# Weight splits over blocks, last stores awaited one stage later, an earlier table load: the seams of a four-stage kernel

## Chip, cores and metric

The kernel runs on one core of a Trainium2 chip. The metric is the time of one execution on the device, in microseconds; lower is better. Five engines work side by side, each through its own list of instructions in order: TensorE (PE, with PEld for its weight loads), VectorE (DVE), ScalarE (ACT), GpSimd (POOL) and SyncE (SP, which here only issues transfers). ACT issues transfers too. They wait for one another by semaphores.

## The reference, cut to what matters

```python
x = x + 0.5 * ffn(layernorm(x))        # base projection + 2 of 8 low-rank experts
x = x + attention(layernorm(x))        # 32 heads, 8 key/value heads, rotary, causal
x = x + 0.5 * ffn(layernorm(x))
...
q = (resid @ Wq)...; k = (resid @ Wk)...; v = (resid @ Wv)...
q = q * cos + _rotate_half(q) * sin
k = k * cos + _rotate_half(k) * sin
att = einsum(q, k) / sqrt(32); causal softmax; ctx = probs @ v
return out @ Wo
```

`x` is 2 x 1024 x 1024 in float32: 2,048 tokens, 16 tiles of 128 tokens. All weights are 1024 wide, Wk and Wv 256 wide.

## The kernel before, in words

Every product is made of float32 operands split in a high and a low part: ACT copies the operand into the type that TensorE takes (the high part), DVE or POOL subtracts it from the original (the low part), and `split_products` (L73) issues three matmuls: high x high, low x high, high x low.

The kernel is four stages in a row, each a `Block` whose end all engines reach before the next one starts:

1. `ffn_stage` "f1" (L100) reads `x`, writes `x1` to memory tile by tile. SP issues the store of a tile (L331) when DVE has added the last part, and at the stage's end (L337) waits until all stores have landed. The first four tiles are also loaded again and normalised into the buffer `early`, and Wq is split.
2. `qkv_stage` "qkv" (L779) computes queries, keys and values in four chunks of 512 tokens (batch b, chunk ch). PE first turns the four early tiles (L959), then `by_pairs` (L965) makes the blocks o = 0 and 1 of the first chunk in two halves of 256 tokens. After that, per chunk: ten output blocks o = 0 to 9 (eight of queries, two of keys) of 24 matmuls each, then four tiles of values. In the blocks o = 1, 3, 5, 7 PE turns a tile of the next chunk at the end of the block (L959, `turn_h`); for that the tile must have been loaded by SP (`load_x`, L894), measured by DVE (L1160, L1164), given its deviation by ACT (L1035) and normalised by DVE (L1172). ACT makes the high part of the turned tile (L1040), DVE the low part (L1178). Each output block passes DVE (L1222, L1224), POOL (L1136), DVE (L1183), ACT (L1047) and POOL (L1130), and ACT stores both parts to memory (L1059). PE needs a bank back after DVE's L1224, four blocks later.
3. `attention_stage` "at" (L1238): sixteen passes of scores, exponentials on ACT (L1670), sums and products.
4. `ffn_stage` "f2" reads `x1` and the attention's result and writes the output.

Wk and Wv are needed from block o = 8 of the first chunk (PE waits for all eight pieces, L1001). Their eight pieces go through two raw buffers (`wkv_raw`): SP loads a piece when POOL is done with the piece two before it (L925 to L927), ACT makes the high part (L1075), POOL the low part (L1124). All eight stand in front of everything else of the stage on ACT and POOL, except that ACT first makes the high parts of the four early tiles:

```python
for j in range(KC):
    act.wait_ge(wkv_loaded[j % WRAW], 32 * (j // WRAW + 1))
    act.activation(wkv_hi[:, j, :], wkv_raw[:, j % WRAW, :], ACT.Copy).then_inc(wkv_hi_done, 1)
```

At the end of the stage, ACT copies each value tile (L1104) and stores it (L1064), calls an exponential on one column so that its table is loaded (L1113), and waits for all stores of queries, keys and values (L1115, L1116).

## Time and profile before

| | us |
|---|---|
| median of 3 runs | 1552.35 (1551.92 to 1552.43) |
| profiled execution | 1550.97 |
| its span, first to last instruction | 1549.2 |
| PE busy in the span | 1504.8 |
| first stage, to about | 260.4 |
| queries, keys, values, to about | 570.2 |
| attention, to about | 1137.6 |
| last stage, to | 1549.2 |

All times below are in microseconds from the span's start. A busy PE counts from the start of a matmul to its modelled end, so starts are the safer thing to compare. "PEq L108" as a releaser stands for the point at which all engines meet at the end of a stage. "Issue" means that the profile shows nothing that the engine waited for.

### The profile page before, as it was taken

How to read it: one execution, taken by the hardware profiler on the slowest of the kernel's cores; microseconds unless marked ns; L12 is line 12 of the kernel's file. 1: busy time of each engine (PE TensorE's matmuls, PEld its weight loads, DVE VectorE, ACT ScalarE, POOL GpSimd, SP SyncE). 2: the span in 40 equal slices, each digit the busy share in tenths (PEclk: the TensorE clock that was granted, in tenths of full speed). 3: DMA queues.
4: the chain of work that ended last, by engine and by line, in shares of the span. 5: the costliest groups of instructions: out<-in, count | busy, mean ns of one | idle time of the engine just before them, and what ended most of it. 6: DMA issues, size and time to landing. Idle time of an engine off the chain costs nothing. (4 is left out here: it accounts for less than half of the span.)

```text
span 1549.2 us, 25938 instructions
## 1 busy us (share of the span) xinstructions
PE 1504.8 (97%) x9184; PEld 1189.7 (77%) x9184; DVE 957.6 (62%) x2726; ACT 569.0 (37%) x1058; POOL 696.2 (45%) x384
## 2 busy tenths in 40 slices
PE   7999998899999989999999999999999999999999
PEld 7999998788888875555555555555479999898988
DVE  6645464465563848888888888888655434343423
ACT  4323233221211136566565556566632212121210
POOL 1322222443334338888888888888612101010100
PEclk9999999999999989999999999999999999999999
DMA  6332324333415172433333344430161212121201
GB/s 234 126 123 86 125 97 147 114 133 98 136 69 158 70 180 53 100 84 82 77 77 76 77 96 101 101 84 23 49 238 48 82 42 82 42 81 41 82 14 41
DMA packets 118725, 146.01 MB, mean 94 GB/s; under 512 B 40896, under 2 KB 77120, under 8 KB 118336
## 3 DMA queue, kind: packets, MB, share of 16 engines
q1 hardware_dynamic: 90304, 121.37, 27.2%
q10 hardware_dynamic: 28304, 23.14, 4.5%
q8 instruction: 66, 1.08, 0.3%
q14 instruction: 51, 0.42, 0.1%
HBM read 95.72 MB, written 53.51 MB: 96 GB/s over the span
## 5 line engine op out<-in xcount | busy, mean ns | idle before, releaser
L1670 ACT ACTIVATE at_probs<-ps 128x512 f32<-128x512 f32 (+1 forms) x640 | 307.1, 557 | 146.2 <-PE ps L1585 145.9
L69 DVE CUSTOM_DVE_ANT_0 ps<-ps,at_score_mask 128x512 f32<-128x512 f32 (+2 forms) x480 | 271.7, 620 | 58.7 <-PE ps L1574 58.1
L348 POOL TENSOR_TENSOR f_x_ring<-f_x_ring,f_half_bias 128x1024 f32<-128x1024 f32 x32 | 78.2, 2445 | 309.3 <-DVE f_h L634 303.1
L1517 POOL TENSOR_TENSOR at_added<-at_added,at_probs 128x2048 f32<-128x2048 f32 (+1 forms) x60 | 210.4, 3506 | 2.2
L1602 PE MATMUL ps<-at_probs,at_vs 128*32 128x512 f32 (+3 forms) x1536 | 157.0, 496 | 0.0
L75 PE MATMUL f_ps<-f_wt_hi,f_hT_hi 128*128 128x400 f32 (+1 forms) x384 | 133.3, 347 | 3.3 <-DVE f_hT_lo L638 3.3
L75 PE MATMUL ps<-f_wt_hi,f_hT_hi 128*128 128x400 f32 (+1 forms) x384 | 131.5, 342 | 0.0
L77 PE MATMUL f_ps<-f_wt_hi,f_hT_lo 128*128 128x400 f32 (+1 forms) x384 | 130.9, 341 | 0.0
L76 PE MATMUL f_ps<-f_wt_lo,f_hT_hi 128*128 128x400 f32 (+1 forms) x384 | 130.6, 340 | 0.0
L76 PE MATMUL ps<-f_wt_lo,f_hT_hi 128*128 128x400 f32 (+1 forms) x384 | 130.2, 339 | 0.0
L77 PE MATMUL ps<-f_wt_hi,f_hT_lo 128*128 128x400 f32 (+1 forms) x384 | 130.0, 338 | 0.0
L69 DVE CUSTOM_DVE_ANT_0 ps<-ps,at_score_mask,at_part_max 128x128 f32<-128x128 f32 (+3 forms) x240 | 120.3, 551 | 1.3 <-issue 0.8
L1497 POOL TENSOR_SCALAR_AFFINE_SELECT at_probs<-at_probs 128x512 f32<-128x512 f32 (+1 forms) x96 | 79.4, 827 | 73.5 <-ACT at_probs L1670 73.5
L673 DVE TENSOR_TENSOR f_x_ring<-ps,f_x_ring 128x512 f32<-128x512 f32 x32 | 21.8, 689 | 138.4 <-PE ps L77 125.1
L1585 PE MATMUL ps<-heads 98*128 98x512 f32 (+3 forms) x288 | 96.7, 383 | 6.4 <-PEq L1557 3.9
L75 PE MATMUL ps<-wide_hi,shared 128*128 128x512 f32 x256 | 101.1, 395 | 1.5 <-DVEq L703 1.0
L1136 POOL TENSOR_TENSOR qkv_rot<-qkv_rot,qkv_sin 128x512 f32<-128x512 f32 x40 | 51.6, 1291 | 111.5 <-DVE qkv_rot L1222 111.5
L77 PE MATMUL ps<-wide_hi,shared 128*128 128x512 f32 x256 | 99.8, 390 | 0.0
L76 PE MATMUL ps<-wide_lo,shared 128*128 128x512 f32 x256 | 99.7, 390 | 0.0
L1585 PEld LDWEIGHTS ps<-heads 98*128 98x128 f32 x288 | 52.9, 196 | 56.2 <-ACT at_probs L1670 30.6
L352 POOL TENSOR_TENSOR wide_lo<-f_wq_raw,wide_hi 128x512 f32 (+1 forms) x16 | 23.6, 1474 | 158.3 <-ACT wide_hi L531 158.3
L1047 ACT ACTIVATE qkv_rope_hi<-qkv_rope 128x512 fp32r<-128x512 f32 x40 | 25.3, 632 | 184.5 <-DVE qkv_rope L1183 171.9
(202 smaller groups left out, 3600.0 us busy)
## 6 DMA issues: line engine op xcount, KB each, us to landing
f_x_ring<-in_L_attn_resid SPq DMA_DIRECT2D x16, 512.0 KB, 3.4
x<-f_x_ring SPq DMA_DIRECT2D x16, 512.0 KB, 2.7
early<-x SPq DMA_DIRECT2D x16, 512.0 KB, 3.3
scr_q_hi<-qkv_rope_hi ACTq DMA_DIRECT2D x32, 256.0 KB, 2.0
scr_q_lo<-qkv_rope_lo ACTq DMA_DIRECT2D x32, 256.0 KB, 2.3
scr_ctx<-at_ctxn SPq DMA_DIRECT2D x32, 256.0 KB, 2.4
shared<-scr_ctx SPq DMA_DIRECT2D x16, 512.0 KB, 4.5
f_x_ring<-x SPq DMA_DIRECT2D x16, 512.0 KB, 3.7
```

The costliest lines, as they stand in the source:

```text
L69: return dve.tensor_tensor_reduce(out=src[:, 0:keys], in0=src[:, 0:keys], in1=mask, scale=1.0, scalar=part_max[:, g, own] if c else -3.0e3 ...
L75: pe.matmul(out, stat_hi, mov_hi, start=start, stop=False)
L76: pe.matmul(out, stat_hi, mov_lo, start=False, stop=False)
L77: return pe.matmul(out, stat_lo, mov_hi, start=False, stop=stop)
L348: pool.tensor_tensor(x_ring[:, u, :], x_ring[:, u, :], half_bias[:], ALU.add).then_inc(bias_added, 1)
L1047: act.activation(rope_hi[:, g % 2, :], rope[:, g % 2, :], ACT.Copy).then_inc(hi_done, 1)
L1136: pool.tensor_tensor(rot[:, g % 2, :], rot[:, g % 2, :], sin[:, cols], ALU.mult).then_inc(sin_done, 1)
L1497: pool.affine_select(out=tile, in_=tile, compare_op=ALU.is_ge, fill=0.0, base=0, pattern=[[0, G], [0, count], [1, P]], channel_multiplier= ...
L1517: pool.tensor_tensor(added[:, heads, :], first, probs[:, (NU * n + u) % PROBS, heads, :], ALU.add).then_inc(added_done, 1)
L1585: last = pe.matmul(score_ps[x % BANKS][:, cols], ks[:, nm, j * P:(j + 1) * P], q_stack(n)[0:KROWS + 2, half, g, at], start=True, stop=True)
L1602: last = pe.matmul(ctx_ps[g * DH:(g + 1) * DH, at], vs[:, n % RING, j, :], probs[:, (NU * n + u) % PROBS, g, cols], start=j == 0, stop=u i ...
L1670: act.activation(probs[:, (NU * n + u) % PROBS, g, cols], score_ps[x % BANKS][:, cols], ACT.Exp, scale=SCALE).then_inc(exp_done, 1)
```

## The change

- The pieces of Wk and Wv are split in the blocks of the first chunk, by ACT and by POOL: pieces 0 and 1 ahead of block o = 0, piece o + 1 ahead of block o, up to o = 6. SP loads tiles 6 and 7 between the pieces 3 and 4 and the pieces 5 and 6 (before: after piece 7).
- The store of the last tile of stage 1 counts on a semaphore of its own (`x_stored`), for which SP waits as its first act in stage 2. `x_ring` is given another place in the memory.
- ACT no longer waits for the value stores at the end of stage 2; SP waits for them in stage 3, after its first three loads. `v_out` outlives the stage.
- The exponential on one column is called ahead of the four value tiles of the last chunk (before: after them).
- Loops of one round are written out.

```diff
--- before.py
+++ after.py
@@ -97,7 +97,7 @@
     return tile[:, :, :].rearrange("p c n -> p (c n)") if len(tile.shape) == 3 else tile[:, :]
-def ffn_stage(nc, name, x_src, x_dst, base_b, consts, ident, chunk_loaded, prep=None, attn=None):
+def ffn_stage(nc, name, x_src, x_dst, base_b, consts, ident, chunk_loaded, prep=None, attn=None, x_stored=None):
@@ -112,6 +112,7 @@
         def sem(n):
             return ctx.enter_context(nc.semaphore(f"{name}_{n}"))
+        x_ring = sb("x_ring", [P, 4, D], F32)
         fw = ffn_weights(nc, ctx, name)
         (wt_hi, wt_lo), (bt_hi, bt_lo) = fw["wt"], fw["bt"]
         if prep:
@@ -126,7 +127,6 @@
         if attn:
             wo_hi, wo_lo = attn["wo"]
             ctxT = [attn["ctxT"][:, par, :, :, :] for par in range(2)]
-        x_ring = sb("x_ring", [P, 4, D], F32)
         half_bias = sb("half_bias", [P, D], F32)
         h = sb("h", [P, D], F32)
         hT_hi = sb("hT_hi", [P, 2, KC, P], F32R)
@@ -328,13 +328,14 @@
                     sp.dma_start(prep["copy"]["wt"][bass.ds(2 * i + u // 2, 1), half, :].rearrange("c p n -> (c p) n"),
                                  prep["ffn_w"][bass.ds(2 * i + u // 2, 1), half, :].rearrange("c p n -> (c p) n")).then_inc(copy_stored, 16)
                 sp.wait_ge(ffn_added, 3 * t + 6)
-                sp.dma_start(x_dst[bass.ds(t * P, P), :], x_ring[:, u, :]).then_inc(stored[u], 16)
+                own = x_stored if prep and isinstance(t, int) and t == NT - 1 else stored[u]
+                sp.dma_start(x_dst[bass.ds(t * P, P), :], x_ring[:, u, :]).then_inc(own, 16)
             if prep:
                 for u in range(2):
                     step(0, u, u, 3)
             run_tiles(sp, step)
             for s in range(4):
-                sp.wait_ge(stored[s], 16 * (NT // 4) + (16 if s == 3 else 0))
+                sp.wait_ge(stored[s], 16 * (NT // 4) + (16 if s == 3 and not prep else 0))
             if prep:
                 sp.wait_ge(copy_stored, 16 * (1 + NT))
@@ -776,7 +777,7 @@
             run_tiles(dve, step)
-def qkv_stage(nc, x_src, wq, early, heads, w, consts, ident, scr):
+def qkv_stage(nc, x_src, wq, early, heads, v_out, w, consts, ident, scr, x_stored, v_stored):
@@ -813,7 +814,6 @@
         rope = sb("rope", [P, 2, HALF], F32)
         rope_hi = sb("rope_hi", [P, 2, HALF], F32R)
         rope_lo = sb("rope_lo", [P, 2, HALF], F32R)
-        v_out = sb("v_out", [P, 2, KV], F32)
@@ -857,7 +857,6 @@
         out_stored = [sem(f"out_stored{s}") for s in range(2)]
         v_done = sem("v_done")
         v_copied = sem("v_copied")
-        v_stored = [sem(f"v_stored{s}") for s in range(2)]
         first_head_loaded = sem("first_head_loaded")
         rest_loaded = sem("rest_loaded")
         mask_ready = sem("mask_ready")
@@ -882,11 +881,15 @@
         def run_chunks(eng, step):
-            with eng.Fori(0, B - 1, 1) as b:
+            for b in range(B):
                 for ch in range(NCH):
-                    step(b, ch, True)
-            for ch in range(NCH):
-                step(B - 1, ch, ch + 1 < NCH)
+                    step(b, ch, b + 1 < B or ch + 1 < NCH)
+
+        def weights_of(b, g):
+
+            if b or g >= KC - 1:
+                return ()
+            return (0, 1) if g == 0 else (g + 1,)
         @block.sync
         def _(sp):
@@ -914,6 +917,7 @@
                     dst = q_stacks[0][KROWS + row:KROWS + row + 1, half * G:(half + 1) * G, :].rearrange("p g t -> p (g t)")
                     sp.dma_start(dst.bitcast(F32), src).then_inc(neg_loaded, 16)
+            sp.wait_ge(x_stored, 16)
             sp.dma_start(cos[:], consts["rope_cos"]).then_inc(const_loaded, 16)
             sp.dma_start(sin[:], consts["rope_sin"]).then_inc(const_loaded, 16)
             for j in range(KC):
@@ -921,13 +925,14 @@
                     sp.wait_ge(h_turned, TC + 1)
                     for slot in range(2):
                         load_x(TC + slot, slot)
+                if j in (WRAW + 2, WRAW + 4):
+                    load_x(TC + j // 2, j // 2 % 2)
                 if j >= WRAW:
                     sp.wait_ge(wkv_lo_done, j - WRAW + 1)
                 for cols, src in ((slice(0, KV), w["Wk"]), (slice(KV, 2 * KV), w["Wv"])):
                     sp.dma_start(wkv_raw[:, j % WRAW, cols], src[j * P:(j + 1) * P, :]).then_inc(wkv_loaded[j % WRAW], 16)
-            with sp.Fori(TC // 2 + 1, NT // 2, 1) as i:
-                for slot in range(2):
-                    load_x(2 * i + slot, slot)
+            for t in range(TC + 4, NT):
+                load_x(t, t % 2)
             sp.wait_ge(v_done, (B * NCH - 1) * TC + 1)
             for s in range(2):
                 sp.wait_ge(out_stored[s], NCH * NO * 16 + 16)
@@ -1070,7 +1075,8 @@
             act.wait_ge(eps_set, 1)
             for t in range(TC):
                 high_hT(0, t, early=True)
-            for j in range(KC):
+
+            def high_weight(j):
                 act.wait_ge(wkv_loaded[j % WRAW], 32 * (j // WRAW + 1))
                 act.activation(wkv_hi[:, j, :], wkv_raw[:, j % WRAW, :], ACT.Copy).then_inc(wkv_hi_done, 1)
@@ -1086,6 +1092,8 @@
                 act.wait_ge(v_done, b * (NCH * TC) + (ch * TC + 1))
                 for o in range(NO):
                     g = ch * NO + o
+                    for j in weights_of(b, g):
+                        high_weight(j)
                     if not more and o and TURN_A in items_of(o):
                         negative(0)
                     if more and o % 2 == 0 and o // 2 < TC:
@@ -1097,6 +1105,8 @@
                     if more and o % 2 == 1 and o // 2 < TC:
                         high_hT(b, (ch + 1) * TC + o // 2)
+                if not more:
+                    act.activation(std[:], eps[:], ACT.Exp)
                 for s in range(TC):
                     t = ch * TC + s
                     act.wait_ge(v_done, b * (NCH * TC) + (t + 2))
@@ -1110,19 +1120,19 @@
                         negative(1)
                     store_v(b, t)
             run_chunks(act, step)
-            act.activation(std[:], eps[:], ACT.Exp)
             for s in range(2):
                 act.wait_ge(out_stored[s], B * NCH * NO * 16 + 16)
-                act.wait_ge(v_stored[s], B * NCH * TC * 8 + 16)
         @block.gpsimd
         def _(pool):
             pool.memset(eps[:], EPS).then_inc(eps_set, 1)
             pool.sem_inc(lo_done, 2)
-            for j in range(KC):
+
+            def low_weight(j):
                 pool.wait_ge(wkv_hi_done, j + 1)
                 pool.tensor_tensor(wkv_lo[:, j, :], wkv_raw[:, j % WRAW, :], wkv_hi[:, j, :].bitcast(F32),
                                    ALU.subtract).then_inc(wkv_lo_done, 1)
+
             pool.wait_ge(const_loaded, CONSTS)
             def low_part(b, g):
@@ -1131,6 +1141,8 @@
                                    ALU.subtract).then_inc(lo_done, 1)
             def chunk_step(b, g):
+                    for j in weights_of(b, g):
+                        low_weight(j)
                     cols = slice((g // NO) * HALF, (g // NO + 1) * HALF)
                     pool.wait_ge(swapped, b * (NCH * NO) + (g + 1))
                     pool.tensor_tensor(rot[:, g % 2, :], rot[:, g % 2, :], sin[:, cols], ALU.mult).then_inc(sin_done, 1)
@@ -1139,7 +1151,7 @@
                     if g % NO == NO - 1:
                         low_part(b, g)
-            with pool.Fori(0, B - 1, 1) as b:
+            for b in range(B - 1):
                 for g in range(NCH * NO):
                     chunk_step(b, g)
             for g in range(NCH * NO):
@@ -1235,7 +1247,7 @@
             run_chunks(dve, step)
-def attention_stage(nc, consts, ident, scr, wo, wo_src, heads, shared, ps):
+def attention_stage(nc, consts, ident, scr, wo, wo_src, heads, shared, ps, v_stored):
@@ -1453,6 +1465,8 @@
             for r in range(2):
                 sp.sem_inc(stacks_loaded[r], LOADS - 16)
                 load_v(r)
+            for stored in v_stored:
+                sp.wait_ge(stored, NT * 8 + 16)
             for stored in ctx_stored:
                 sp.sem_inc(stored, 16)
@@ -1793,15 +1807,19 @@
     chunk_loaded = [whole.enter_context(nc.semaphore(f"chunk_loaded{c}")) for c in range(KC + 1)]
     wide = [whole.enter_context(nc.sbuf_tensor(f"wide_{part}", [P, KC, D], F32R)) for part in ("hi", "lo")]
     over = ExitStack()
+    x_stored = whole.enter_context(nc.semaphore("x_stored"))
+    v_stored = [whole.enter_context(nc.semaphore(f"v_stored{s}")) for s in range(2)]
     with ExitStack() as ctx:
         early = ctx.enter_context(nc.sbuf_tensor("early", [P, 4, D], F32))
-        ffn_stage(nc, "f1", x, x1, base_b, consts, ident, chunk_loaded, prep={"wq": wide, "early": early, "Wq": ins["L0_attn_Wq"], "copy": copy, **raw})
+        ffn_stage(nc, "f1", x, x1, base_b, consts, ident, chunk_loaded, prep={"wq": wide, "early": early, "Wq": ins["L0_attn_Wq"], "copy": copy, **raw},
+                  x_stored=x_stored)
         heads = over.enter_context(nc.sbuf_tensor("heads", [P, 2, KC, HALF], F32R, side="right"))
-        qkv_stage(nc, x1, wide, early, heads, attn_w, consts, ident, scr)
+        v_out = over.enter_context(nc.sbuf_tensor("v_out", [P, 2, NKV * DH], F32, side="right"))
+        qkv_stage(nc, x1, wide, early, heads, v_out, attn_w, consts, ident, scr, x_stored, v_stored)
     with ExitStack() as ctx:
         shared = ctx.enter_context(nc.sbuf_tensor("shared", [P, 2, 2, KC, P], F32R))
         ps = ctx.enter_context(nc.psum_tensor("ps", [P, 8, HALF], F32))
-        attention_stage(nc, consts, ident, scr, wide, ins["wo_rows"], heads, shared, ps)
+        attention_stage(nc, consts, ident, scr, wide, ins["wo_rows"], heads, shared, ps, v_stored)
         over.close()
         ffn_stage(nc, "f2", x1, y, base_b, consts, ident, chunk_loaded,
                   attn={"wo": wide, "ctxT": shared, "ps": ps, "ffn_w": copy["wt"], "ffn_bt": copy["bt"],
```

## Rows read from the trace of the kernel before

**Rows 1.** The page: granted clock in tenths, 40 slices.

```profile
PEclk9999999999999989999999999999999999999999
```

**Rows 2.** Timeline of PE, 257 to 296 us: start, us, instruction, [idle before <-releaser].

```profile
259.19 0.27 PE L77 MATMUL f_ps<-f_bt_hi,f_lowT_lo 128*128 128x224 f32 x1
...
263.62 5.35 PE L959 MATMUL qkv_ps<-ident,early 128*128 128x128 f32 x32 [4.16 <-PEq L108]
...
269.40 0.39 PE L75 MATMUL qkv_ps<-heads,wide_hi 128*128 128x256 f32 x1 [0.43 <-DVE heads L1178]
...
280.90 0.28 PE L77 MATMUL qkv_ps<-heads,wide_lo 128*128 128x256 f32 x1
...
288.38 1.94 PE L959 MATMUL qkv_ps<-ident,early 128*128 128x128 f32 x8 [7.19 <-issue]
```

**Rows 3.** Windows: length, PE, PEld, DVE, ACT, POOL busy, PEclk, DMA, GB/s.

```profile
264.00:264.50 0.50, 0.50 (x5) 0.50 (x4) 0.00 (x0) 0.00 (x0) 0.00 (x0) 0.50 0.50 66
...
267.00:267.50 0.50, 0.50 (x6) 0.50 (x5) 0.50 (x1) 0.43 (x1) 0.00 (x0) 0.71 0.97 377
...
291.00:292.00 1.00, 1.00 (x5) 0.83 (x4) 1.00 (x1) 0.00 (x0) 0.52 (x1) 0.91 0.07 25
```

**Rows 4.** Timelines of DVE and ACT at the first normalised tile.

```profile
272.26 1.28 DVE L1160 BATCH_NORM_STATS2 qkv_stats<-early 128x6 f32<-128x512 f32 x2 [0.65 <-DMA early<-x]
...
286.81 1.47 DVE L1172 TENSOR_SCALAR early<-early,qkv_mv,qkv_rstd 128x1024 f32<-128x1024 f32 x1
...
286.29 0.28 ACT L1035 ACTIVATE qkv_std<-qkv_mv,qkv_eps 128x1 f32<-128x1 f32 x1
```

**Rows 5.** Groups of ACT by line, and timeline of POOL, 262 to 290 us.

```profile
L1075 ACT ACTIVATE qkv_wkv_hi<-qkv_wkv_raw 128x512 fp32r<-128x512 f32 x8 | 4.9, 632 | 11.5 <-DMA qkv_wkv_raw<-in_L_attn_Wv 11.5
...
280.24 2.50 POOL L1124 TENSOR_TENSOR qkv_wkv_lo<-qkv_wkv_raw,qkv_wkv_hi 128x512 fp32r<-128x512 f32 x2 [2.47 <-ACT qkv_wkv_hi L1075]
```

**Rows 6.** Timeline and waits of the queue of SP, 225 to 300 us.

```profile
260.07 0.35 SPq L331 DMA_DIRECT2D x<-f_x_ring  x1
...
SPq L337 <- DMA x<-f_x_ring: 2.3, 1, 2.3
```

**Rows 7.** Timelines of DVE and PE at a later turned tile.

```profile
322.74 0.81 DVE L1172 TENSOR_SCALAR early<-early,qkv_mv,qkv_rstd 128x1024 f32<-128x1024 f32 x1
...
325.96 1.03 PE L959 MATMUL qkv_ps<-ident,early 128*128 128x128 f32 x8
```

**Rows 8.** Timelines of PE and ACT, 535 to 578 us.

```profile
561.03 0.28 PE L75 MATMUL qkv_ps<-qkv_wkv_hi,qkv_hT 128*128 128x256 f32 x1
...
566.67 0.28 PE L77 MATMUL qkv_ps<-qkv_wkv_hi,qkv_hT 128*128 128x256 f32 x1
...
570.84 4.18 PE L1585 MATMUL ps<-heads 98*128 98x512 f32 x10 [3.89 <-PEq L1557]
...
558.64 0.39 ACT L1104 ACTIVATE qkv_v_out<-qkv_ps 128x256 f32<-128x256 f32 x1 [0.43 <-PE qkv_ps L77]
...
567.40 0.38 ACTq L1064 DMA_DIRECT2D scr_v<-qkv_v_out  x1
...
567.81 1.28 ACT L1113 ACT_TABLE_LOAD   x1 [0.44 <-ACT qkv_v_out L1104]
```

**Rows 9.** Timeline of PE, 570 to 582 us, and one window.

```profile
574.82 0.41 PE L1574 MATMUL ps<-heads,wide_lo 96*128 96x128 f32 x1
...
581.00:581.50 0.50, 0.50 (x3) 0.48 (x2) 0.38 (x2) 0.46 (x2) 0.50 (x1) 0.68 1.22 280
```

**Rows 10.** Timeline of PE and windows in the first 60 us.

```profile
13.21 0.43 PE L75 MATMUL f_ps<-f_wt_hi,f_hT_hi 128*128 128x360 f32 x1 [2.37 <-DVE f_hT_lo L638]
...
57.43 0.30 PE L434 MATMUL f_ps<-ident,f_low_s 128*128 128x128 f32 x1 [1.68 <-DVE f_hT_lo L638]
...
15.00:16.50 1.50, 1.50 (x6) 1.50 (x6) 1.35 (x4) 0.56 (x3) 0.00 (x0) 0.50 0.69 158
...
58.50:60.00 1.50, 1.50 (x10) 1.50 (x9) 1.27 (x3) 0.89 (x2) 0.00 (x0) 1.00 0.00 0
```

## Prediction

> **What bounds the kernel now.** I read the page first. PE is busy 1504.8 of 1549.2 us, 97%, and the granted clock is 9 tenths or more in 39 of the 40 slices; the one with an 8 is the fifteenth, 542 to 581 us, and holds a seam [rows 1]. So a change that does not shorten PE's own work can only gain where PE stands still or runs at the lower clock. The waits of PE name few places, and I went to the timeline of PE around them. At the seam between the first and the second stage the last matmul starts at 259.19 and ends at 259.46, and the first transpose starts at 263.62: 4.16 us of nothing. Then come 32 transposes, a pause of 0.43, the pair blocks from 269.40 to 281.18, and then a second hole of 7.19 us before the transposes at 288.38 [rows 2]. The windows show the clock. It is at half (1.2 of 2.4 GHz) at 264.0 and is given back inside 267.0 to 267.5; it is at half again after the second hole and comes back early in the window 291 to 292, whose mean is 0.91 [rows 3]. At the seam between the second and the third stage PE stands still from 566.95 to 570.84 [rows 8], and the clock is then at half until inside 581.0 to 581.5 [rows 9]. The seam to the last stage has no such wait, and between the seams the waits of PE name nothing of size. Time won at a seam is therefore kept: everything behind it is PE's own chain, moved to the left.
>
> **The second hole (edit 1).** PE stands at the turning of tile 4. Who is late? DVE measured that tile at 272.26, as soon as it was loaded, but could normalise it only at 286.81, because ACT gave the deviation at 286.29 [rows 4]. ACT was busy with the eight weight pieces: eight copies of 632 ns are 4.9 us, and it waited 11.5 us for their loads in between, since each load waits for POOL to free a buffer, 1.25 us a piece [rows 5]. In the new order only pieces 0 and 1 stand ahead of the deviation. Both had landed when ACT reached them before. The deviation then follows the measuring, which ends at about 273.8 even if the tile is loaded no sooner than now; with 0.3 for ACT, 0.2 for a reciprocal and 0.8 for the normalising, the tile stands at about 275.3. PE needs it at 277.5 or later (below). The hole goes: 7.2 us.
>
> The tail goes with it. From 288.38 to 291.1 PE worked at half clock, 2.7 us in which it did 1.35 us of work [rows 2, 3]: 1.4 us.
>
> What the eight pieces cost in their new place: per block 0.63 us more of ACT, 1.25 more of POOL. A block lasts PE about 5.9 us by the two pair blocks, which take 11.8. POOL has two more operations of about the same length in it, so 3.8 of 5.9; ACT has far less. Both sit ahead of the block's own waits, where POOL stands idle for DVE. Queued behind them are the sine product on POOL, and on ACT the deviation and the high part of the turned tile, which PE needs for the next turn. I looked for how much room that loop has: tile 7's normalising starts at 322.74, is done at 323.55, and PE turns it at 325.96 [rows 7]. That is 2.4 us of room, and one ACT copy plus one POOL piece is 1.9 if nothing of them hides. I count them at nothing; without cover they would still fit. Piece 7 is done in block 6, a whole block before PE asks for it. The loads of tiles 6 and 7, now between the pieces, make SP wait for the normalised tiles 4 and 5 before it loads pieces 4 and 6; the first is ready at about 275, the second a block later, and a piece has about two blocks between POOL's release and ACT's use.
>
> **The first seam (edit 2).** SP issues the last store at 260.07, is through with it at 260.42, and waits 2.3 us until it lands; PE starts at 263.62, 0.9 us after that [rows 2, 6]. SP's waits name this store alone there; all others were issued with the tiles before. Without the wait, PE starts 0.9 us after 260.42, at 261.3: 2.3 us. The wait itself moves to SP in stage 2, where cosine, sine, pieces 0 and 1 and tiles 4 and 5 queue behind it. SP's first transfer therefore starts at about 262.8 and no later than now, and what hangs on it (tile 4, needed by 277.5) has the room shown above. Bounds: 0, if something else is as late as the store, and 2.3. I take 2.3, since the row names the store.
>
> PE's hole is then 259.46 to 261.3, 1.8 us. Does the clock fall? This kernel has two holes near that size: after 2.37 us (up to 13.21) the clock was at half in 15.0 to 16.5, after 1.68 us (up to 57.43) it stayed full [rows 10]. 1.8 is nearer to the second, so I take full clock. The transposes then take 1.03 for eight where they take 1.94 at half [rows 2, 7]. The pair blocks wait for the first two of the four tiles to be split, so the gain is at least one such difference, 0.9, and at most two, 1.8: 1.3 us. The pair blocks then start at 265.7 and end at 277.5, 11.8 later as now. If the clock falls after all, the 1.3 is lost, and as much half clock as at this seam now (264 to 267.3 [rows 3]) costs up to 1.7 more.
>
> **The second seam (edits 3 and 4).** ACT issues the last value store at 567.40 for 0.38 us, loads the table from 567.81 to 569.09, and waits for the store. PE starts at 570.84 [rows 8]. Both the table and the landing must leave this place to gain anything, and both do. ACT arrives at 567.8; with the 0.9 of the first seam PE starts at 568.7, with a little more for the different first instructions at 568.8: 2.0 us. Bounds 0 and 2.2. The moved table load takes 1.28 and its column 0.2 in front of the copy at 558.64 [rows 8], which then ends at about 560.4. The third value tile, which takes that bank again, starts at 561.03 [rows 8], so it is free. SP waits for the value stores behind three loads, and nothing that it issues after them is due in the first pass.
>
> The Trainium skill, "ScalarE: Activation LUTs", section "What ACT_TABLE_LOAD costs", counts a drain on top of the load, 2.66 us in all. By that figure the copy would end at about 561.8, PE would stand still for some 0.8, and the sum would be 13.9 in place of 14.7. The row shows the activation right behind the 1.28 us.
>
> How long is the clock at half in attention? Now until 581.3. PE is paced by ACT up to 574.82 and works without pause from there [rows 9], so half clock costs at most half of 6.5 us, 3.2. The hole shrinks to 1.9 us, but matmuls paced by ACT follow it, unlike the two cases above. Bounds 0 and 3.2; I think it falls mostly as now and take 0.5.
>
> **Sum.** 7.2 + 1.4 + 2.3 + 1.3 + 2.0 + 0.5 = 14.7 us. The profiled execution took 1550.97, so 1536.3, with a span of 1534.5. The median lies 1.4 above the profiled one: 1537.6.
>
> **Rivals.**
> - *Full clock at both seams:* the 0.5 becomes 3.2, and with the bounds of the rest the gain is 17.6: 1534.7. For it: both holes shrink below 2 us. Against it: the fall after 2.37 [rows 10]. The Trainium skill, "TensorE: Matmul & The Clock Gate", section "HAM oscillation — how this bites in real kernels", has the clock fall only after idle gaps longer than both of these. By that rule this rival is the forecast, 1534.7; the fall after 2.37 us speaks against taking it whole. 15%.
> - *The clock falls at the first seam as well:* 14.7 less 3.0 is 11.7: 1540.7. 15%.
> - *Something else holds the seams:* the stores are not what the engines wait for last, and 2.3 and 2.0 are lost: 1541.9. Against it: the wait of SP is 2.3 long and names the store. 8%.
> - *Half a hole stays:* tile 4 is still late, by a load that starts later or a piece that has not landed: 3 to 5 us, 1541 to 1543. 5%.
> - *Slower:* the pieces no longer run as a batch, and each puts its load on PE's path. The loop tile, deviation, normalise, turn has 2.4 us of room. From there on every block pays. ACT waited about 3 us for a landing; with 0.6 and 1.25 for the splits that is 4.9 a block, less 1.2 of room, over seven blocks 26: 1552.35 - 14.7 + 26 = 1563.6; it decides from 2.1 a block on (14.7 over seven). Against it: a piece has two blocks of time to land. 3%.
>
> The forecast itself, 1536 to 1539.5, gets 54%. The range from 1534.5 to 1542 holds that and the first three rivals, over 8 in 10. A measurement of this kernel can tell about 0.2%, 3.1 us, from no change. Faster by more than that: 0.95; within it: 0.02; slower: 0.03.
>
> **What would show it.** In the profile of the changed kernel: no wait of PE at the turning of tile 4, the transposes there directly behind the pair blocks; PE's holes at the seams 1.8 and 1.9 us; transposes of about 1.03 for eight at the first seam; POOL and ACT splitting weights up to about 310, with no PE wait between. A PE wait at a turn or at the first key block, a first transpose later than 262, or a half clock in the pair blocks would make me wrong.

## The result, and the profile after

The changed kernel takes 1538.83 us in the median of four runs (1536.21 to 1541.13), and the kernel before, on the same chip, 1552.13 (1551.16 to 1552.43). The ratio is 0.9915, with a 95% interval of 0.9894 to 0.9936: 13.3 us faster. The predicted time was 1537.6. The profiled execution took 1536.89 with a span of 1535.1, against a forecast of 1536.3 and 1534.5.

First, PE's timeline of the changed kernel, at the first seam and at the turns of tiles 4, 5 and 7 (start, us, instruction, idle time before it):

```profile
258.12 0.27 PE L77 MATMUL f_ps<-f_bt_hi,f_lowT_lo 128*128 128x224 f32 x1
260.31 5.35 PE L964 MATMUL qkv_ps<-ident,early 128*128 128x128 f32 x32 [1.92 <-PEq L108]
265.42 0.36 PE L75 MATMUL qkv_ps<-heads,wide_hi 128*128 128x256 f32 x1
...
276.90 0.29 PE L77 MATMUL qkv_ps<-heads,wide_lo 128*128 128x256 f32 x1
277.02 1.03 PE L964 MATMUL qkv_ps<-ident,early 128*128 128x128 f32 x8
...
289.12 1.04 PE L964 MATMUL qkv_ps<-ident,early 128*128 128x128 f32 x8
...
313.30 1.04 PE L964 MATMUL qkv_ps<-ident,early 128*128 128x128 f32 x8
```

The page's row of the granted clock, beside [rows 1], has no slice below 9 any more:

```profile
PEclk9999999999999999999999999999999999999999
```

PE's timeline set beside [rows 2]: the hole at the seam is 1.92 us where it was 4.16, and the second hole, 7.19 us before the turn of tile 4, has gone; the eight transposes stand directly behind the last matmul of the pair blocks and take 1.03, not 1.94. But the 32 transposes at the seam take 5.35 us, as before. The windows say why (length, busy time of PE, PEld, DVE, ACT and POOL, granted clock, DMA share, GB/s):

```profile
261.00:261.50 0.50, 0.50 (x6) 0.50 (x5) 0.00 (x0) 0.02 (x1) 0.00 (x0) 0.82 0.24 90
261.50:262.00 0.50, 0.50 (x5) 0.50 (x4) 0.00 (x0) 0.50 (x1) 0.00 (x0) 0.50 0.00 0
...
264.50:265.00 0.50, 0.50 (x6) 0.50 (x5) 0.50 (x1) 0.24 (x1) 0.00 (x0) 0.77 1.03 410
...
558.00:558.50 0.50, 0.50 (x2) 0.25 (x1) 0.00 (x0) 0.50 (x2) 0.00 (x0) 0.78 1.26 197
558.50:559.00 0.50, 0.50 (x2) 0.29 (x1) 0.00 (x0) 0.50 (x3) 0.00 (x0) 0.50 1.16 183
...
565.00:565.50 0.50, 0.50 (x5) 0.26 (x2) 0.00 (x0) 0.00 (x0) 0.00 (x0) 0.89 1.14 225
```

A window whose mean lies between 0.50 and 1.00 holds the change of level. The clock was at half from 261.3 to 264.7 and from 558.3 to 565.1. DVE and ACT at the first normalised tile, which answer to [rows 4, 5]:

```profile
272.35 0.21 DVE L1176 BATCH_NORM_AGGREGATE qkv_mv<-qkv_stats 128x2 f32<-128x12 f32 x1
...
273.12 0.81 DVE L1184 TENSOR_SCALAR early<-early,qkv_mv,qkv_rstd 128x1024 f32<-128x1024 f32 x1
...
267.28 1.22 ACT L1081 ACTIVATE qkv_wkv_hi<-qkv_wkv_raw 128x512 fp32r<-128x512 f32 x2 [0.55 <-DMA qkv_wkv_raw<-in_L_attn_Wv]
272.60 0.29 ACT L1040 ACTIVATE qkv_std<-qkv_mv,qkv_eps 128x1 f32<-128x1 f32 x1 [4.10 <-DVE qkv_mv L1176]
272.81 0.63 ACT L1081 ACTIVATE qkv_wkv_hi<-qkv_wkv_raw 128x512 fp32r<-128x512 f32 x1
```

ACT now waits for DVE's measuring and gives the deviation 0.04 us after it ends (272.56). Tile 4 is normalised at 273.93, and PE turns it at 277.02. The other pieces follow one a block; POOL's eighth starts at 307.37. SP's queue at the first seam, its timeline and then its waits, beside [rows 6]:

```profile
259.00 0.35 SPq L332 DMA_DIRECT2D x<-f_x_ring  x1
261.65 0.34 SPq L921 DMA_DIRECT2D qkv_cos<-in_rope_cos  x1
...
265.70 0.81 SPq L900 DMA_DIRECT2D early<-x  x2
```

```profile
SPq L921 <- DMA x<-f_x_ring: 1.6, 1, 1.6
```

The wait for the last store is now SP's alone: it lands at 261.65, when PE has been at work for 1.3 us. The second seam, PE and ACT, beside [rows 8]:

```profile
554.30 0.28 PE L77 MATMUL qkv_ps<-qkv_wkv_hi,qkv_hT 128*128 128x256 f32 x1
556.56 0.93 PE L1599 MATMUL ps<-heads 98*128 98x512 f32 x3 [1.98 <-PEq L1571]
...
546.12 1.28 ACT L1109 ACT_TABLE_LOAD   x1 [0.27 <-ACT qkv_rope_hi L1052]
547.41 0.20 ACT L1109 ACTIVATE qkv_std<-qkv_eps 128x1 f32<-128x1 f32 x1
547.52 0.37 ACT L1114 ACTIVATE v_out<-qkv_ps 128x256 f32<-128x256 f32 x1
...
555.03 0.38 ACTq L1069 DMA_DIRECT2D scr_v<-v_out  x1
```

The hole went from 3.89 to 1.98 us, and the table load lies among the value tiles.

Measured between the same instructions of PE, the two profiled executions differ by this ledger:

| stretch | before | after | gain | predicted |
|---|---|---|---|---|
| start to the last matmul of stage 1 | 259.19 | 258.12 | 1.1 | 0 |
| to the first transpose | 4.43 | 2.19 | 2.2 | 2.3 |
| to the first pair matmul | 5.78 | 5.11 | 0.7 | 1.3 |
| to the turn of tile 4 | 18.98 | 11.60 | 7.4 | 7.2 |
| to the turn of tile 5 (301.81; 289.12) | 13.43 | 12.10 | 1.3 | 1.4 |
| to the last matmul of stage 2 | 264.86 | 265.18 | -0.3 | 0 |
| to the first score | 4.17 | 2.26 | 1.9 | 2.0 |
| to the last products of attention (1125.15; 1110.44) | 554.31 | 553.88 | 0.4 | 0.5 |
| to the end | 424.05 | 424.66 | -0.6 | 0 |
| sum | 1549.2 | 1535.1 | 14.1 | 14.7 |

### The profile page after: what moved, and what is told of

It reads as the page before. It is cut to its first block and busy times, and to the rows that moved or that the text cites. A ratio compares the mean times of both kernels' runs of the same rounds, so it can differ in the third digit from the quotient of the medians.

```text
span 1535.1 us, 25888 instructions
## 1 busy us (share of the span) xinstructions
PE 1501.5 (98%) x9184; PEld 1186.6 (77%) x9184; DVE 957.4 (62%) x2726; ACT 568.7 (37%) x1058; POOL 697.3 (45%) x384
## 3 DMA queue, kind: packets, MB, share of 16 engines
q8 instruction: 66, 1.08, 0.3%
```

## The experiments

All are timed against the kernel before on the same chip, with four to six runs of each version. Gains by the ratio are (1 - ratio) x 1552; the ratio rests on all runs, so it can differ from the ratio of the two medians by up to a thousandth and a half, 2 us. For the three parts of the change both are given.

**The same kernel again.** No edit.

> The changed kernel once more, against the kernel before on the same chip. Theory A (each part is worth the piece of PE's standstill that it removes; the clock at the seams is decided anew in each run): 1536 to 1541, ratio 0.990 to 0.993, single runs up to 4 us apart, where the kernel before has 1. Theory B (one state of the chip, slower or faster for the whole job): the runs of this kernel lie within 1 us of each other, as those of the kernel before do.

1539.31 us, ratio 0.9913 (0.9894 to 0.9933), single runs from 1536.59 to 1544.24. The profiled one took 1540.42, span 1538.7, 3.6 longer than the first profile. Its windows:

```profile
559.50:560.00 0.50, 0.50 (x2) 0.27 (x2) 0.00 (x0) 0.50 (x2) 0.00 (x0) 0.53 0.94 172
...
572.50:573.00 0.50, 0.50 (x3) 0.41 (x2) 0.50 (x1) 0.28 (x1) 0.00 (x0) 0.50 0.00 0
573.00:573.50 0.50, 0.50 (x3) 0.43 (x2) 0.41 (x3) 0.34 (x2) 0.00 (x0) 0.81 0.00 0
```

Half clock lasts from 559.5 to 573.2 here, 13.7 us, where the first profile has 6.8. The ledger puts 3.5 of the 3.6 us into attention (557.38 for 553.88). Another 1.1 come from stage 1 (last matmul at 259.21, not 258.12), and other stretches give back 1.0. So identical code differs by several us, most of it from how long the clock stays at half. The mean granted clock that each timed run of this kernel left says the same without a profile: the five runs at 0.995 to 0.997 took 1536.21 to 1538.21 us, the five at 0.992 to 0.994 took 1540.42 to 1544.24.

The median lies in A's range and B is refuted, but A's "up to 4 us apart, where the kernel before has 1" is not borne out: the single runs lie 7.7 us apart, and those of the kernel before on this chip 7.1 (1550.54 to 1557.66). On this chip the spread is no property of the change.

**The split alone**, with both seams as before:

```diff
-                own = x_stored if prep and isinstance(t, int) and t == NT - 1 else stored[u]
-                sp.dma_start(x_dst[bass.ds(t * P, P), :], x_ring[:, u, :]).then_inc(own, 16)
+                sp.dma_start(x_dst[bass.ds(t * P, P), :], x_ring[:, u, :]).then_inc(stored[u], 16)
...
-                sp.wait_ge(stored[s], 16 * (NT // 4) + (16 if s == 3 and not prep else 0))
+                sp.wait_ge(stored[s], 16 * (NT // 4) + (16 if s == 3 else 0))
...
-            sp.wait_ge(x_stored, 16)
...
-                if not more:
-                    act.activation(std[:], eps[:], ACT.Exp)
...
+            act.activation(std[:], eps[:], ACT.Exp)
             for s in range(2):
                 act.wait_ge(out_stored[s], B * NCH * NO * 16 + 16)
+                act.wait_ge(v_stored[s], B * NCH * TC * 8 + 16)
```

> The weight splits over the blocks alone; the last store, the value stores and the table load as in the kernel before. Theory A: the second hole of 7.2 us and its half-clock tail of 1.4 go, so 1543.6 (8.6 less than before), with PE's holes at the two seams at 4.2 and 3.9 us as before. Theory C (the splits cost something in their new place, on ACT or POOL): less than 7 us gained, and PE waits at a turn of a tile between 277 and 330. Theory D (all of the gain is in the splits, the seams are worth nothing): as fast as the changed kernel, 1538 to 1539.

1546.16 us, ratio 0.9958 (0.9943 to 0.9973); the profiled run took 1543.3. The holes of the seams are back at 4.16 and 3.90 us, and PE has none at the turn of tile 4. From the first pair matmul to that turn it takes 11.6, as in the full change. The row of the turn has no idle time before it:

```profile
281.55 1.04 PE L962 MATMUL qkv_ps<-ident,early 128*128 128x128 f32 x8
```

The gain is 6.5 us by the ratio and 5.3 between the medians (1551.5 before), that of the spans 7.6 with a stage 1 that was 0.9 later. That bears A's mechanism out; its median of 1543.6 was 2.6 too low. The gain is under the 7 us of theory C, but the sign that C names, a wait of PE at a turn, is nowhere between 277 and 330. The other place of `x_ring` and the written-out loops are in this version too, and no run has them alone.

**The first seam back**, with the first three parts of that diff:

> The changed kernel, but the last store of the first stage is awaited at that stage's end again. Theory A: PE's hole at the first seam is 4.2 us again, 2.3 more than in the changed kernel, and the clock is at half in the transposes as it was there too: 2.3 us slower than the changed kernel, about 1541. Theory D: no slower than the changed kernel.

1543.57 us, ratio 0.9942 (0.9927 to 0.9956). The first hole is 4.16, and half clock lasts 6.8 us behind it (3.4 in the first profile):

```profile
262.83 6.56 PE L962 MATMUL qkv_ps<-ident,early 128*128 128x128 f32 x32 [4.16 <-PEq L108]
```

Against the same kernel again, on the same chip, this seam is worth 0.0029 of 1552, 4.5 us, by the ratios and 4.3 by the medians, where A had 2.3. The hole is 2.2 of it, and the way from the first transpose to the first pair matmul 1.2 more (6.32 for 5.11).

**The second seam back**, with the rest of that diff:

> The changed kernel, but the value stores are awaited at the second stage's end, after the exponential table's load, as before. Theory A: PE's hole at the second seam is 3.9 us again, 1.9 more than in the changed kernel; with the time at half clock in attention, 10 us before and 7 in the changed kernel's profile, 2 to 4 us slower, 1540 to 1543. Theory D: no slower than the changed kernel.

1541.46 us, ratio 0.9924 (0.9909 to 0.9939), second hole 3.89. The seam is worth 1.7 us by the ratios, 2.2 by the medians and 1.9 by the holes. The median lies in A's range, but the intervals of the ratios overlap almost whole, so only the hole shows it. The clock did not fall at the first seam in this profile. The 32 transposes and the wait behind them then took 4.63 us to the first pair matmul, where the first profile has 5.11 and the kernel before 5.78.

**Only the table load back** at the end of the stage, and, apart, **only the wait for the value stores back**:

```diff
-                if not more:
-                    act.activation(std[:], eps[:], ACT.Exp)
...
+            act.activation(std[:], eps[:], ACT.Exp)
             for s in range(2):
```

```diff
                 act.wait_ge(out_stored[s], B * NCH * NO * 16 + 16)
+                act.wait_ge(v_stored[s], B * NCH * TC * 8 + 16)
```

> The changed kernel with only the exponential table loaded behind the last value tile again; the value stores are still awaited in stage 3. Theory A (both the table and the store had to leave the end of the stage): ACT issues the last store, loads the table for 1.28 us and reads one column for 0.2, so it reaches the end of the stage 1.3 to 1.5 us later, and PE's hole at the second seam is 3.3 to 3.5 us in place of 2.0. Median 1540.3 to 1541.5 where the clock behaves as in the other runs. Theory B (only the landing of the store held the seam, the table ran beside something else): the hole stays at 2.0 us, no difference.

> The changed kernel with only the wait for the value stores back at the end of stage 2; the table is still loaded ahead of the four value tiles. Theory A: the store lands some 2 us after it is issued, whatever the table does, so PE's hole is 3.4 to 3.9 us; the table alone is worth 0 to 0.5 us without the moved wait. Theory B (the two are worth about half of the second seam each): hole about 2.9 us.

1539.06 (0.9902 to 0.9928) and 1540.26 (0.9905 to 0.9931): by time, neither can be told from the full change. The timelines of PE can tell them, the table first, then the wait:

```profile
558.41 4.38 PE L1598 MATMUL ps<-heads 98*128 98x512 f32 x10 [3.25 <-PEq L1570]
```

```profile
561.08 4.39 PE L1600 MATMUL ps<-heads 98*128 98x512 f32 x10 [3.93 <-PEq L1572]
```

The hole is 3.25 us with the table there, 3.93 with the landing there, 3.90 with both and 1.98 with neither. The two run side by side, and the later one counts. Either alone keeps most of the hole, so half of this edit would have shortened the hole by 0 to 0.7 us. A is right in both in its mechanism. Its holes of 3.3 to 3.5 and 3.4 to 3.9 us were each missed by less than 0.1, and the first median lies 1.2 below its range of 1540.3 to 1541.5.

**Twice the work of POOL per piece**, to see how near the splits are to PE's path. The second subtraction's result is not used.

```diff
+                pool.tensor_tensor(early[:, 3, (j % 2) * 512:(j % 2 + 1) * 512], wkv_raw[:, j % WRAW, :], wkv_hi[:, j, :].bitcast(F32), ALU.subtract)
                 pool.tensor_tensor(wkv_lo[:, j, :], wkv_raw[:, j % WRAW, :], wkv_hi[:, j, :].bitcast(F32),
```

> The changed kernel with one more subtraction of a weight piece on POOL, 1.25 us, ahead of each piece's own; its result is used by nobody. Theory A (the pieces are hidden in the blocks, with 2.4 us of room in the loop that feeds the turns): no difference from the changed kernel beyond its own spread, 1536 to 1541, and no wait of PE at a turn. Theory C (the pieces are already on PE's path): about 1.25 us for each of the seven blocks, up to 9 us slower, with PE waiting at the turns.

1539.88 us, ratio 0.9923 (0.9902 to 0.9943). PE waits at no turn, though POOL works without pause from 276.3 to 284.3. DVE's normalising of tile 5 starts at 284.29 for 0.81, PE turns it at 288.77: 3.7 us of room. Later ones take 1.37 and have less:

```profile
309.99 1.37 DVE L1185 TENSOR_SCALAR early<-early,qkv_mv,qkv_rstd 128x1024 f32<-128x1024 f32 x1
```

PE turns that tile at 312.91, 1.55 us after it is ready. The rival "slower" was far off: even doubled, the work stays hidden.

**Fillers on PE.** The holes left are 1.92 and 1.98 us, and the clock still falls. These three versions let PE turn the identity in addition, into a bank that nobody reads: eight times at the end of stage 1; the same and eight at the end of stage 2; the same and two behind each of the first eight scores.

```diff
+            if prep:
+                for _ in range(8):
+                    pe.transpose(ps[:, 7, 0:P], ident[:], ident[:])
...
+            pe.wait_ge(cos_done, B * NCH * NO + 4)
+            for _ in range(8):
+                pe.transpose(ps[:, 2, 0:P], ident[:], ident[:])
...
                     scores(0, u, g)
+                    for _ in range(2):
+                        pe.transpose(slot_ps[SLOTS - 1][:, 0:P], ident[:], ident[:])
```

> The changed kernel with eight transposes of the identity on PE at the end of the first stage, while it would wait for the others; nobody reads their result. PE's hole at the first seam shrinks from 1.9 to about 1.0 us. Theory E (the spread of the changed kernel and the missing gain at the first seam come from the clock, which falls there in spite of the shorter hole): the clock stays full at the first seam, the 32 transposes take 4 us instead of 5.4, about 1.5 us faster than the changed kernel, 1537.5 median. Theory F (the clock has nothing to do with it): as fast as the changed kernel or 0.5 slower.

> As the last one, with eight such transposes at the end of the second stage too. Theory E: PE's hole at the second seam is about 1.0 us. If the hole alone makes the clock fall there, it stays full and attention starts 3.4 to 6.8 us faster: 1532 to 1534, with a spread of 1 us. If the thin work behind the hole (scores paced by the exponentials) does it, the clock falls all the same: 1537.5, with the spread of 4 us. Theory F: as fast as the changed kernel.

> As the last one, with two such transposes behind each of the first eight scores of attention, where PE is paced by ACT. Theory E with the thin work as the cause: the clock stays full through both seams, 1532 to 1534, spread 1 us, and no half clock from 555 to 575. Theory F: up to 2 us slower than the changed kernel, for the added work.

> The version with filler transposes at both seams and behind the first eight scores once more, to see whether its time is reproduced. Theory A (the fillers keep the clock full at both seams, and that is worth the half-clock time of some 7 to 14 us in attention, halved): median 1533.5 to 1536.5, no stretch of half clock at either seam. Theory B (1534.8 was a lucky draw of a clock that falls at random): about 1538, with a stretch of half clock behind the second seam.

| version | us | ratio (95%) | holes | half clock, seam 1 and 2 |
|---|---|---|---|---|
| seam 1 filled | 1538.89 | 0.9914 (0.9897-0.9931) | 1.05, 1.98 | 0, 10.2 |
| both filled | 1539.91 | 0.9912 (0.9894-0.9930) | 1.05, 1.11 | 0, 6.8 |
| scores too | 1534.84 | 0.9888 (0.9865-0.9910) | 1.08, 1.11 | 0, 0 |
| scores too, again | 1536.19 | 0.9894 (0.9880-0.9908) | 1.05, 1.14 | 0, 0 |

With seam 1 filled the clock stayed full there, as E said, but its 1.5 us did not come: the way from the first transpose to the first pair matmul is 4.63 us, 0.5 less than in the changed kernel, and the median is no lower. Without fillers the same seam kept full clock in three profiles of six, so four of four with them is weak evidence that they are the reason.

With both seams filled PE stood still for only 1.11 us at the second, and yet the clock fell four microseconds later:

```profile
559.64 0.94 PE L1605 MATMUL ps<-heads 98*128 98x512 f32 x3 [1.11 <-PEq L1577]
560.79 2.67 PE L1605 MATMUL ps<-heads 98*128 98x512 f32 x7 [0.22 <-ACT at_probs L1690]
```

The windows of the same profile:

```profile
563.50:564.00 0.50, 0.50 (x5) 0.50 (x4) 0.13 (x1) 0.50 (x3) 0.10 (x1) 0.66 0.85 307
...
565.00:566.00 1.00, 1.00 (x5) 0.86 (x5) 0.81 (x4) 0.64 (x2) 0.00 (x0) 0.50 1.03 205
```

So the branch of E that blames the hole alone (1532 to 1534) is refuted, and the median lies 2.4 above the 1537.5 of the other. With transposes between the scores the clock stayed full (timeline, then windows):

```profile
557.80 0.47 PE L1605 MATMUL ps<-heads 98*128 98x512 f32 x1 [1.11 <-PEq L1577]
558.11 0.38 PE L1653 MATMUL ps<-ident 128*128 128x128 f32 x2
558.25 0.48 PE L1605 MATMUL ps<-heads 98*128 98x512 f32 x1
558.56 0.38 PE L1653 MATMUL ps<-ident 128*128 128x128 f32 x2
```

```profile
559.00:561.00 2.00, 2.00 (x16) 1.86 (x15) 0.00 (x0) 2.00 (x6) 0.45 (x1) 1.00 1.10 185
561.00:565.00 4.00, 4.00 (x31) 2.90 (x31) 2.25 (x14) 2.71 (x8) 2.16 (x4) 1.00 0.98 229
```

The first score to the last products of attention took 551.90 and 551.96 us in the two profiles of this version, against 553.88 and 557.38 in those of the changed kernel. The medians are 4.0 and 2.6 us below the 1538.83 of the changed kernel. The intervals of the ratios overlap, but the second set of runs repeats the first, and both medians lie below every other one here. It is the best version found, about 17 us below the kernel before. E's 1532 to 1534 with a spread of 1 us was too good: the first median is 1534.84, the spread 4.8.

For the repeat, A's range held the median, and neither profile shows half clock at a seam. But the fillers do not hold the clock in every run. The mean granted clock of the eight timed runs is 0.999 in five (1533.07 to 1535.41 us) and 0.997 in three (1537.26 to 1537.83). The two profiles are of runs at 0.999, and their only half clock is 3.4 us near the start of stage 1. A mean of 0.997 is, as an estimate, (1 - 0.997) x 2 x 1536 = 9 us at half. Where those three runs had it is not known. None of the ten runs of the changed kernel comes above 0.997. So the thin work behind the hole (scores that wait for ACT) is a likely part of the cause, not shown to be all of it: with both holes filled, one profile with bare scores has a fall and two with transposes between them have none.

## Why the prediction was right, and where it was not

The median of 1538.83 lies 1.2 above the 1537.6 of the forecast and inside its 1536 to 1539.5. The span accounts for 0.6 of the 1.2. The rest is the 1.4 us by which the median was taken to lie above the profiled execution: it was 1.9 here, and in the repeat of the same kernel the median lay 1.1 below. That it came out inside 1536 to 1539.5 is in part luck: of the ten runs of this kernel five lie there, and five lie at 1540.4 to 1544.2.

**The second hole and its tail** (7.2 + 1.4; measured 7.4 + 1.3). The deviation of tile 4 had stood behind the eight pieces on ACT, and it now follows the measuring. The split alone shows the same 11.6 us from the pair blocks to the turn.

**The splits in the blocks cost nothing.** This was right, and with a margin: the room from the normalised tile to its turn is 3.1, 3.3, 2.8 and 2.4 us for tiles 4 to 7, and one more subtraction of 1.3 us per piece did not use it up.

**The hole of the first seam** (2.3; measured 2.2). Putting the wait back puts the 4.16 us back.

**The clock at the first seam.** This is the step that failed: "1.8 is nearer to the second, so I take full clock". After 1.92 us of idle PE the clock was at half in both profiles of the changed kernel and in that of the store wait back, for 3.4 us each time. It stayed full in those of the second seam back, the table back and the doubled split, with the same hole of 1.9 us in front. So neither answer was right for every run.

The two holes that the choice leaned on do not decide it either. The one of 2.37 us near the start is followed by a fall in twelve of the thirteen profiles and by none in that of the doubled split. Before it PE did eight transposes in 1.91 us, as slowly as at half clock, so it is no likeness of a seam. The one at 57 us is 1.4 to 2.6 us long and was followed by full clock in eleven of the thirteen. But the clock fell in it with seam 1 filled (2.38 us) and with both filled (2.42), and stayed full after 2.44 and 2.60. The first of the two falls, timeline and window:

```profile
58.53 0.45 PE L435 MATMUL f_ps<-ident,f_low_s 128*128 128x128 f32 x1 [2.38 <-DVE f_hT_lo L642]
```

```profile
58.50:59.00 0.50, 0.47 (x2) 0.50 (x3) 0.00 (x0) 0.00 (x0) 0.00 (x0) 0.50 0.00 0
```

The size of the term was nearly right, and the loss by a fall was overrated. With full clock the transposes are followed by a wait of 0.95 us for DVE, and the way to the first pair matmul is 4.63 us, 1.2 less than the 5.78 before, where the term had 1.3. With the clock falling 1.0 and 1.2 us behind the first transpose (changed kernel, twice), in place of 0.3 before, it is 5.11. The term measured 0.7 that way, not nothing; with a fall 0.5 us behind (store wait back) it is 5.53. The further 1.7 that I had set for a fall did not come, since the clock was back at 264.7, before the pair blocks. That is why the rival "the clock falls at the first seam as well", which occurred, did not bring its 1540.7.

**The second seam** (2.0; measured 1.9). Right, and for the reason given: both things had to leave. Nothing was seen of the drain that the Trainium skill counts beside the table load ("ScalarE: Activation LUTs", "What ACT_TABLE_LOAD costs"): the load starts 0.27 us after the activation before it, the column's activation 1.29 us after the load does, and the copy 0.11 us after that.

**The clock in attention** (0.5; measured 0.4 in this pair of profiles). The term was right for them, and too sure as a constant. Set the distance from the first score to the last products against the time at half clock behind the second seam, over the thirteen profiles:

| half clock, us | distance, us | profiles |
|---|---|---|
| 0 | 551.90, 551.96 | fillers at the scores, twice |
| 6.8 | 553.88, 554.89 | changed; both seams filled |
| 10.2 | 554.31 to 555.09 | before; split alone; second seam back; table back; seam 1 filled |
| 13.7 | 556.80 to 557.38 | changed again; first seam back; split twice |
| 17.1 | 557.48 | store wait back |

The versions differ in the seam before these stretches, so the rows are not the same code throughout. The whole term is worth up to 5.6 us, and the length of the hole does not order it: after the same 1.98 us the same kernel drew 6.8 and 13.7. The lower bound of 0 does not hold: in the second profile of the changed kernel this stretch is 3.1 us longer than before (557.38 for 554.31). A draw of 13.7 in place of 6.8 puts the kernel at 1540.4. The range held this only because its upper end came from other rivals. What decides the draw stays open.

**The other rivals.** Nothing else held the seams (1541.9), no half of the second hole stayed (1541 to 1543), and the splits did not reach PE's path (1563.6); the ledger and the doubled split show all three. The split alone is the case of the first, seams that give nothing. It took 1546.16, not 1541.9: the rival had left the gains of the clock, 1.3 and 0.5, in the sum although the holes that it keeps are the long ones, and of the 8.6 for the second hole 5.3 to 6.5 came in the timed runs. The range would not have held that case.

**Full clock at both seams** (1534.7). No profile of the changed kernel shows this, but with the fillers it came about in both profiles, at medians of 1534.84 and 1536.19. The Trainium skill's rule on idle gaps ("TensorE: Matmul & The Clock Gate", "HAM oscillation — how this bites in real kernels") does not agree with these rows if idle gaps are all that counts. By it, gaps of 1.92 and 1.98 us are too short for a fall, and the clock fell after both, and after a gap of 1.11 us that scores at ACT's pace followed.

**What was not in the sum.** The profiled executions also differ by 1.1 us in stage 1, by 0.3 in the last part of stage 2 and by 0.6 in the last stage. The first cannot be credited to the change: the last matmul of stage 1 started between 258.1 and 262.0 us in the twelve profiles that have the new place of `x_ring`, and at 259.2 before. The 0.6 has one visible part, a wait of 0.7 of PE for DVE's part of `shared`, which the repeat of the same kernel does not show (423.98 from the last products to the end). The 0.3 was not traced.

The experiments add up: by the ratios 6.5 for the split, 4.5 and 1.7 for the seams, together 12.7 of 13.2 to 13.5; by the medians of that chip 5.3, 4.3 and 2.2, together 11.8 of 12.2. By the widths of the intervals, each part is uncertain by 2 to 4 us, so the proof of each is its hole, not its time.

## What to carry to other kernels

Where PE is busy 97% of the span, go through its few holes. Name for each the last thing that releases it, and measure gains between two instructions of PE, since the whole time varies by more than a seam is worth (single runs of identical code lay 7.7 us apart). When two things end a stage side by side, moving only one of them gains next to nothing; the time reads "no difference", and only the hole tells. After a short hole the clock can fall or not from run to run: quote a forecast that rests on it with both levels, and where the matmuls behind the hole wait for another engine, try a few idle transposes between them. The mean granted clock of each run tells cheaply whether they held it.

## What the runs showed of the hardware

- The clock fell to half after idle times of PE of 1.92, 1.98 and 1.11 us, and at other times stayed full after 1.92 us in front of the same 32 transposes. Around another hole, at 57 us, it fell with 2.38 and 2.42 us and stayed full with 2.44 and 2.60.
- It stayed at half for 6.8 to 17.1 us behind the second seam, although PE had next to no pause there (8.93 of the 9 us from 561 to 570 in the version with the store wait back, at 0.50).
- Sixteen extra transposes in the place where PE waits for ACT's exponentials went with full clock in both profiles and, by the mean granted clock of 0.999, in five runs of eight. They cost next to nothing: the first ten scores take 3.71 and 3.70 us with them and 3.67 without (both seams filled), and 551.9 us for attention is the least of all versions.
- PE starts the next stage 0.96 us after SP is through with its last issue at the first seam (259.35 to 260.31), and 1.15 us after ACT is at the second (555.41 to 556.56).
